# Full attention's scores copied negated out of their PSUM ring together with the maximum, with score products two slots ahead and entropy sums two slots behind

## The chip, the core and the metric

The kernel runs on one core of one Trainium2 chip. The time is the device time of one launch in microseconds (us), from the first to the last instruction of the program and what the runtime puts around them. Smaller is better. The core has five engines that run their own instruction queues in order and meet only at semaphores: TensorE (PE in the rows, its weight loads PEld), VectorE (DVE), ScalarE (ACT), GpSimd (POOL) and SyncE (SP, here the queue that issues the DMAs).

## The reference

Eight sequences of 512 tokens with 128 features pass through four residual blocks: causal attention with ALiBi, a gated feed-forward network, a second attention ("hybrid") and the feed-forward network again. The change lies in the second attention. It first needs, for all 16 heads, the whole softmax of 512 x 512 scores, only to rank the tokens:

```
scores = softmax(einsum('bhqd,bhkd->bhqk', q, k) * scale)
entropy   = -sum(scores * log(clip(scores, 1e-8)), axis=-1)
max_attn  = scores.max(axis=-1)
influence = scores.sum(axis=-2)
importance = -entropy.mean(1)*0.4 + max_attn.mean(1)*0.3 + influence.mean(1)*0.3
_, idx = top_k(importance, 51)
# then attention of all queries over the 51 picked tokens and 64 compressed ones
```

With s a score, M the maximum of its row and Z the sum of exp(s - M), the clipped logarithm of the softmax is max(s - M - ln Z, ln 1e-8). The kernel therefore forms, per query row, the sum of exp(s - M) times max(s, threshold), where the threshold is M + ln(1e-8 Z), and corrects it afterwards with a few small operations.

## The kernel before

The scores of one sequence are cut into **main tiles**: one tile is one head and one block of 128 queries, 128 partitions by 512 keys in float32, which is exactly one PSUM bank. A sequence has 16 x 4 = 64 main tiles, the eight sequences have 512. Everything in the kernel is placed on a time axis of **slots**, written out by hand in a table of constants (`FIRST`, `M_AT`, `A1_AT`, ...). Slot g holds main tile n = g - FIRST - M_AT, and beside it whatever pieces of the other stages are due: the main tiles of sequence b run while sequence b+1 is in its causal attention's second pass and its feed-forward network, b+2 in the causal first pass, and b-1 and b-2 in their small attention and last feed-forward network. The pattern thus repeats every 64 slots. Each engine walks the same slots in its own loop and waits at semaphores; no engine is bound to be in the same slot as another beyond what the semaphores ask.

For one main tile n the work is:

- TensorE, `full_scores` (L1263, product at L1268): a bf16 product into bank n % 3 of a ring of three banks (`RING`, `RN` = 3). It is issued `LEAD` = 1 slot early, that is in slot n - 1, as the first thing of that slot. From the fourth tile on it waits for `s_bn`, the semaphore of the entropy sums, of tile n - 3 (L1265).
- VectorE, first in slot n: the negated maximum of each row out of the bank, `nmB` (L1068, a TENSOR_REDUCE), which frees ScalarE's next step.
- ScalarE, in slot n: exp(s - M) out of the bank into one of eight SBUF buffers `E` (these lie in the tensor `setup`, by which the rows name them), with the sum Z as accumulator output (L827); then ln(1e-8 Z) (L830).
- GpSimd: the threshold, lnZ - nmB (L695).
- VectorE, at the end of slot n + 1, behind everything else of that slot: `entropy` (L974, operation at L978), a SCALAR_TENSOR_TENSOR that reads the scores out of the bank a second time and E from SBUF, with the sum as accumulator output. It releases the bank.
- After each fourth tile VectorE inverts Z (L1086), and one slot later TensorE adds E times 1/Z to the influence sums of the sequence (`influence`, L1271, L1276).

The other stages use banks 3, 4, 5 and 7, taken in turns that a table fixes. VectorE's parts in them are the maxima of the causal first pass (L933 to L940) and of the small attention (L946), divisions (L956, L958), residuals and layer statistics; ScalarE's are the exponentials (L813, L909), copies out of PSUM (L742) and the SiLU with its table loads (L800, L801); GpSimd's are the normalisations (L667) and the splitting of numbers into bf16 parts (L673, L678, L683, L687), all on SBUF data.

## Time and profile before

| | |
|---|---|
| median of 3 runs | 1926.42 us (1925.96 to 1930.85) |
| profiled execution, its own time | 1930.84 us |
| span of the profiled execution | 1928.7 us |
| mean granted TensorE clock | 0.692 of full speed |
| busy: PE, PE weight loads | 1487.1 us (77%), 652.0 us (34%) |
| busy: VectorE, ScalarE, GpSimd | 1223.3 us (63%), 1001.2 us (52%), 389.4 us (20%) |

Busy is the time in which an engine has an instruction in work. What is left is idle time, and the profile names for it the instruction that ended the wait. No engine is near 100%, so the waits between engines matter as much as the work. Idle time counts only on the engine that sets the pace of a stretch; which one that is changes within the 64 slots, so the profile is read by stretches of one repetition. The first main tile's maximum starts at 230 us and the last at 1779 us; before and behind lie the first sequence's earlier stages and the last one's final stages.

### The profile page before, as it was taken

To read this page: it belongs to the slowest core of one execution; us is meant where nothing else is said; L and a number is where in the kernel's file an instruction comes from. 1 tells how busy PE (TensorE), PEld (TensorE's weight loads), DVE (VectorE), ACT (ScalarE), POOL (GpSimd) and SP (SyncE) were. 2 spreads that over 40 slices of the span, in tenths; PEclk is the share of its full clock that TensorE was granted. 3 is DMA by queue.
4 is the path that set the end of the run, shared out by engine and by line. 5 is a ranking of instruction groups with operands and counts; after the bars stand their busy time and mean duration, and the time that the engine had idled before them with its cause. 6 is when DMAs were issued, how large, how long until landed. Compare 5 with 4: busy or idle time off the path is not lost.

```text
span 1928.7 us, 25028 instructions
## 1 busy us (share of the span) xinstructions
PE 1487.1 (77%) x7949; PEld 652.0 (34%) x7949; DVE 1223.3 (63%) x3203; ACT 1001.2 (52%) x2478; POOL 389.4 (20%) x900
## 2 busy tenths in 40 slices
PE   1786797888788788788788878878878878678645
PEld 1333432343334333344234333334334322321312
DVE  1503556877787477856787478857786577787211
ACT  1051376457556555656556655565654657546122
POOL 3102301330133012310233023301221012110100
PEclk9566577659666777677766876677766867665555
DMA  2110210122012110122012111211011002200100
GB/s 59 31 47 11 57 34 17 42 50 41 6 50 52 23 23 14 45 46 45 14 39 52 28 19 36 53 26 33 14 34 36 12 14 45 27 13 12 17 8 5
DMA packets 65619, 59.17 MB, mean 31 GB/s; under 512 B 11936, under 2 KB 63184, under 8 KB 65488
## 3 DMA queue, kind: packets, MB, share of 16 engines
q1 hardware_dynamic: 65488, 57.58, 14.2%
q8 instruction: 63, 1.03, 0.2%
q14 instruction: 68, 0.56, 0.1%
HBM read 39.10 MB, written 18.27 MB: 30 GB/s over the span
## 4 chain that ended last, share of the span: by engine, by line
PE 50%; DVE 22%; ACT 15%; issue 7%; POOL 3%; DMA 2%; SPq 0%; ACTq 0%; POOLq 0%; DVEq 0%
PE bank L1276 8%; PE bank L1316 7%; DVE junk L978 5%; ACT setup L827 4%; PE bank L1268 4%; PE bank L1244 3%; PE bank L1221 3%; PE bank L1299 3%; DVE nm L946 3%; ACT pT L813 2%; DVE nmB L1068 2%; DVE nm L933 2%; PE bank L1259 2%; PE bank L1251 2%; PE bank L1200 2%
## 5 line engine op out<-in xcount | busy, mean ns | idle before, releaser
L827 ACT ACTIVATE setup<-bank,nmB 128x512 f32<-128x512 f32 x512 | 350.4, 684 | 340.7 <-DVE nmB L1068 339.5
L978 DVE SCALAR_TENSOR_TENSOR junk<-bank,thr,setup 128x512 f32<-128x512 f32 x512 | 379.2, 741 | 96.5 <-POOL thr L695 92.6
L1068 DVE TENSOR_REDUCE nmB<-bank 128x1 f32<-128x512 f32 x512 | 351.1, 686 | 111.5 <-PE bank L1268 111.3
L1268 PE MATMUL bank<-k_stacks,q_stacks 48*128 48x512 bf16 x512 | 254.5, 499 | 151.8 <-DVE junk L978 150.1
L695 POOL TENSOR_TENSOR thr<-lnZ,nmB 128x1 f32<-128x1 f32 x512 | 96.7, 190 | 1223.5 <-ACT lnZ L830 1223.2
L813 ACT ACTIVATE pT<-bank 128x512 f32<-128x512 f32 x320 | 174.3, 590 | 133.5 <-PE bank L1229 132.1
L1276 PE MATMUL bank<-setup,rz 128*1 128x512 f32 x1024 | 203.0, 879 | 0.0
L1268 PEld LDWEIGHTS bank<-k_stacks,q_stacks 48*128 48x128 bf16 x512 | 49.9, 98 | 384.2 <-DVE junk L978 285.3
L1221 PE MATMUL bank<-q_stacks,k_stacks 55*128 55x384 bf16 (+3 forms) x512 | 138.9, 346 | 36.6 <-ACT pT L813 30.7
L933 DVE TENSOR_REDUCE nm<-bank 128x4 f32<-128x512 f32 x128 | 86.5, 687 | 65.8 <-PE bank L1196 65.8
L909 ACT ACTIVATE p<-bank 115x512 f32<-115x512 f32 x128 | 75.1, 587 | 81.9 <-PE bank L1435 81.8
L1435 PE MATMUL bank<-s_stacks,kcst 51*115 51x512 bf16 x128 | 76.0, 594 | 51.0 <-DVE o L958 28.4
L830 ACT ACTIVATE lnZ<-Z 128x1 f32<-128x1 f32 x512 | 103.9, 203 | 16.1
L1200 PE MATMUL bank<-k_stacks,q_stacks 52*128 52x384 bf16 (+2 forms) x384 | 96.0, 364 | 12.9 <-DVE nm L933 9.6
L1244 PE MATMUL bank<-pT,vA 128*9 128x512 f32 (+3 forms) x1024 | 104.9, 511 | 0.2 <-ACT pT L813 0.2
L1316 PE MATMUL bank<-xnT,wuT 128*128 128x512 f32 x96 | 83.0, 961 | 25.8 <-DVE gated L972 23.8
L827 ACT ACTIVATION_READ_ACCUMULATOR setup<-bank,nmB 128x1 f32 x512 | 101.8, 199 | 0.0
L667 POOL TENSOR_SCALAR xn<-x,mv,rstd 128x128 f32<-128x128 f32 x128 | 100.1, 794 | 3.3
L1229 PE MATMUL bank<-maskr,maskw 64*128 64x128 bf16 (+1 forms) x640 | 91.4, 227 | 0.0
L1192 PE MATMUL bank<-k_stacks,q_stacks 52*128 52x128 bf16 x512 | 68.4, 275 | 29.3 <-DMA k_stacks<-part_dram 17.3
L956 DVE RECIPROCAL rzo<-bank 128x16 f32<-128x16 f32 x64 | 15.7, 245 | 113.0 <-PE bank L1251 113.0
L946 DVE TENSOR_REDUCE nm<-bank 128x4 f32<-128x460 f32 x128 | 74.9, 629 | 16.2 <-PE bank L1310 15.8
(195 smaller groups left out, 2327.9 us busy)
## 6 DMA issues: line engine op xcount, KB each, us to landing
part_dram<-part SPq DMA_DIRECT2D x16, 768.0 KB, 3.2
q_stacks<-part_dram SPq DMA_DIRECT2D x192, 64.0 KB
k_stacks<-part_dram SPq DMA_DIRECT2D x192, 64.0 KB
s_stacks<-part_dram SPq DMA_DIRECT2D x48, 128.0 KB
x<-in_L_attn_a_x_dram SPq DMA_DIRECT2D x8, 256.0 KB, 7.2
x_dram<-x SPq DMA_DIRECT2D x8, 256.0 KB, 2.2
x<-x_dram SPq DMA_DIRECT2D x8, 256.0 KB, 2.9
out_dram<-x SPq DMA_DIRECT2D x8, 256.0 KB, 2.2
```

The lines of the kernel that those rows point to most:

```text
L813: act.activation(pT[:, js[0]:js[0] + len(js), c * T:c * T + WIDTH[c]], bank[3 + u % 2][:, :].rearrange("p (j q) -> p j q", j=len(js)), ACT ...
L827: act.activation(E[:, n % NE, :], RING[n % RN][:, :], ACT.Exp, bias=nmB[mb % 2][:, h, t:t + 1], accum_out=Z[mb % 2][:, h, t:t + 1]).then_i ...
L933: last = dve.tensor_reduce(nm[0][:, :, h], bank[k][:, :].rearrange("p (t k) -> p t k", t=NT), AX_X, ALU.max, negate=True)
L946: dve.tensor_reduce(nm[1][:, :, h], bank[k][:, 0:NT * NK].rearrange("p (t k) -> p t k", t=NT), AX_X, ALU.max, negate=True).then_inc(s_free ...
L978: dve.scalar_tensor_tensor(out=junk[:, :], in0=RING[n % RN][:, :], scalar=thr[mb % 2][:, h, t:t + 1], in1=E[:, n % NE, :], op0=ALU.max, op ...
L1068: dve.tensor_reduce(nmB[mb % 2][:, h, t:t + 1], RING[n % RN][:, :], AX_X, ALU.max, negate=True).then_inc(s_bm, 1)
L1200: last = pe.matmul(bank[k][:, at:at + t * P], qst[0][0:A_SC, h, t * P:(t + 1) * P], kst[0][0:A_SC, h, 0:t * P], start=True, stop=True)
L1221: pe.matmul(bank[k][:, first:first + w], kst[0][0:A_MX, h, j * P:(j + 1) * P], qst[0][0:A_MX, h, j * P:T], start=not squares, stop=True, s ...
L1244: last = pe.matmul(bank[5][QROWS * j:QROWS * j + HD + 1, k * P:T], vA[:, k, HPQ * g + j, :], pT[:, j, c * T + at:c * T + at + T - k * P], ...
L1268: pe.matmul(RING[n % RN][:, :], qst[1][0:B_SC, h, t * P:(t + 1) * P], kst[1][0:B_SC, h, :], start=True, stop=True).then_inc(s_bs, 1)
L1276: last = pe.matmul(INFL[QROWS * t:QROWS * t + 1, :], rz[mb % 2][:, h, t:t + 1], E[:, (NT * h + t) % NE, :], start=(h == 0), stop=(h == H - 1))
L1316: pe.matmul(bank[7][:, :], w, xnT[u][:, :], start=True, stop=True).then_inc(s_full[7], 1)
```

## The change

Five things are changed.

1. VectorE's first operation of a main tile becomes one TENSOR_SCALAR that reads the bank, writes the scores times -1 to one of four SBUF buffers `negs`, and leaves the minimum of them (the negated maximum, as before) as accumulator output in `nmB`. From the fifth tile on it also waits for the exponentials of tile n - 4, which read the same buffer.
2. ScalarE's exponentials and VectorE's entropy operation read `negs` from SBUF instead of the bank: the first with scale -1, the second with the minimum against a negated threshold. Signs follow in GpSimd's threshold and in two small operations for each sequence.
3. TensorE's product for tile n waits for the copy of tile n - 3, not for its entropy sum.
4. `LEAD` goes from 1 to 2: the products are issued two slots ahead.
5. The entropy operation moves from one slot behind its tile to two (`STT_LAG` = 2).

```diff
+        NS = 4
+        negs = [sb(f"negs{i}", [P, T]) for i in range(NS)]
...
-        LEAD = 1
+        LEAD = 2
+        STT_LAG = 2
...
-                        pool.tensor_tensor(thr[mb % 2][:, h, t:t + 1], lnZ[mb % 2][:, h, t:t + 1],
-                                           nmB[mb % 2][:, h, t:t + 1], ALU.subtract).then_inc(s_bt, 1)
+
+                        pool.tensor_tensor(thr[mb % 2][:, h, t:t + 1], nmB[mb % 2][:, h, t:t + 1],
+                                           lnZ[mb % 2][:, h, t:t + 1], ALU.subtract).then_inc(s_bt, 1)
...
-                        act.activation(E[:, n % NE, :], RING[n % RN][:, :], ACT.Exp, bias=nmB[mb % 2][:, h, t:t + 1],
+                        act.activation(E[:, n % NE, :], negs[n % NS][:, :], ACT.Exp, scale=-1.0,
+                                       bias=nmB[mb % 2][:, h, t:t + 1],
                                        accum_out=Z[mb % 2][:, h, t:t + 1]).then_inc(s_be, 1)
...
-                    dve.scalar_tensor_tensor(out=junk[:, :], in0=RING[n % RN][:, :], scalar=thr[mb % 2][:, h, t:t + 1],
-                                             in1=E[:, n % NE, :], op0=ALU.max, op1=ALU.mult,
+                    dve.scalar_tensor_tensor(out=junk[:, :], in0=negs[n % NS][:, :], scalar=thr[mb % 2][:, h, t:t + 1],
+                                             in1=E[:, n % NE, :], op0=ALU.min, op1=ALU.mult,
...
-                        dve.tensor_reduce(nmB[mb % 2][:, h, t:t + 1], RING[n % RN][:, :], AX_X, ALU.max, negate=True
-                                          ).then_inc(s_bm, 1)
+                        if n >= NS:
+                            dve.wait_ge(s_be, n - NS + 1)
+
+                        dve.tensor_scalar(negs[n % NS][:, :], RING[n % RN][:, :], -1.0, None, ALU.mult, ALU.min,
+                                          accum_out=nmB[mb % 2][:, h, t:t + 1]).then_inc(s_bm, 1)
...
-                    if before:
-                        entropy(*before)
+                    lagging = main_tile(g - STT_LAG)
+                    if lagging:
+                        entropy(*lagging)
...
                     if n >= RN:
-                        pe.wait_ge(s_bn, n - RN + 1)
+                        pe.wait_ge(s_bm, n - RN + 1)
```

VectorE's queue in the first main tiles of the first sequence (bank0 to bank2 are the ring, negs0 to negs3 the new buffers, Z0 and rz0 the sums and their inverses). Before:

```order
171 L978 SCALAR_TENSOR_TENSOR junk,acc0<-bank2,thr0,setup 128x512
172 L1068 TENSOR_REDUCE nmB0<-bank1 128x1
173 L1086 RECIPROCAL rz0<-Z0 128x4
174 L978 SCALAR_TENSOR_TENSOR junk,acc0<-bank0,thr0,setup 128x512
175 L1068 TENSOR_REDUCE nmB0<-bank2 128x1
176 L978 SCALAR_TENSOR_TENSOR junk,acc0<-bank1,thr0,setup 128x512
```

The same place in the changed kernel:

```order
170 L983 SCALAR_TENSOR_TENSOR junk,acc0<-negs1,thr0,setup 128x512
171 L1076 TENSOR_SCALAR negs0,nmB0<-bank1 128x512
172 L1094 RECIPROCAL rz0<-Z0 128x4
173 L983 SCALAR_TENSOR_TENSOR junk,acc0<-negs2,thr0,setup 128x512
174 L1076 TENSOR_SCALAR negs1,nmB0<-bank2 128x512
175 L983 SCALAR_TENSOR_TENSOR junk,acc0<-negs3,thr0,setup 128x512
```

Behind the inversion, tile 4 has just been read (bank1, negs0). Before, the entropy operation that follows takes tile 3, the one directly ahead; now it takes tile 2 (negs2).

TensorE's queue in the second pass of the causal attention (L1221, then L1230, are its score products, L1276, then L1285, the influence, L1244, then L1253, the weighing). Before:

```order
380 L1276 MATMUL bank6<-setup,rz0 1x512 x4
381 L1221 MATMUL bank3<-q_stacks,k_stacks 128x256 x2
382 L1229 MATMUL bank3<-maskr,maskw 128x2x64 x2
383 L1221 MATMUL bank4<-q_stacks,k_stacks 128x256 x2
384 L1229 MATMUL bank4<-maskr,maskw 128x2x64 x2
385 L1244 MATMUL bank5<-pT,vA 9x384 x4
386 L1244 MATMUL bank5<-pT,vA 9x128 x4
387 L1268 MATMUL bank0<-k_stacks,q_stacks 128x512
```

The same place in the changed kernel:

```order
380 L1277 MATMUL bank0<-k_stacks,q_stacks 128x512
381 L1285 MATMUL bank6<-setup,rz0 1x512 x4
382 L1230 MATMUL bank3<-q_stacks,k_stacks 128x256 x2
383 L1238 MATMUL bank3<-maskr,maskw 128x2x64 x2
384 L1230 MATMUL bank4<-q_stacks,k_stacks 128x256 x2
385 L1238 MATMUL bank4<-maskr,maskw 128x2x64 x2
386 L1253 MATMUL bank5<-pT,vA 9x384 x4
387 L1253 MATMUL bank5<-pT,vA 9x128 x4
388 L1277 MATMUL bank1<-k_stacks,q_stacks 128x512
```

The product into bank0 now stands ahead of a whole slot of other work that it stood behind.

## Rows read from the trace of the kernel before

**Rows 1.** The page's part 5, whole run: VectorE's two operations of a main tile and the product.

```profile
L978 DVE SCALAR_TENSOR_TENSOR junk<-bank,thr,setup 128x512 f32<-128x512 f32 x512 | 379.2, 741 | 96.5 <-POOL thr L695 92.6
L1068 DVE TENSOR_REDUCE nmB<-bank 128x1 f32<-128x512 f32 x512 | 351.1, 686 | 111.5 <-PE bank L1268 111.3
L1268 PE MATMUL bank<-k_stacks,q_stacks 48*128 48x512 bf16 x512 | 254.5, 499 | 151.8 <-DVE junk L978 150.1
```

**Rows 2.** Three stretches: busy us (count) of PE, PEld, DVE, ACT, POOL; PEclk, DMA.

```profile
1022.00:1110.00 88.00, 73.19 (x464) 35.82 (x463) 50.44 (x145) 54.87 (x134) 16.13 (x37) 0.77 0.22 44
1110.00:1154.00 44.00, 33.62 (x186) 14.56 (x186) 34.06 (x84) 25.61 (x63) 9.26 (x23) 0.75 0.12 21
1154.00:1234.00 80.00, 66.46 (x346) 27.15 (x346) 67.84 (x171) 44.14 (x114) 22.39 (x48) 0.67 0.13 30
```

**Rows 3.** The first two of these stretches for L1068 alone.

```profile
1022.00:1110.00 88.00, 16.50 (x24) 0.77 0.22 44
1110.00:1154.00 44.00, 10.98 (x16) 0.75 0.12 21
```

**Rows 4.** Waits of TensorE and VectorE from 1022 to 1110 us: total, times, longest.

```profile
PE bank L1268 <- DVE junk L978: 6.6, 3, 3.7
...
DVE nmB L1068 <- PE bank L1268: 12.8, 11, 2.5
DVE rz L1086 <- ACT setup L827: 6.1, 2, 4.6
DVE junk L978 <- POOL thr L695: 5.4, 7, 1.4
```

**Rows 5.** The same waits from 1110 to 1154 us.

```profile
PE bank L1268 <- DVE junk L978: 4.9, 4, 2.2
...
DVE junk L978 <- POOL thr L695: 3.5, 6, 1.3
...
DVE nmB L1068 <- PE bank L1268: 1.2, 1, 1.2
```

**Rows 6.** The same waits from 1154 to 1234 us.

```profile
PE bank L1268 <- DVE junk L978: 6.3, 7, 2.2
...
DVE nm L933 <- PE bank L1196: 5.9, 7, 1.9
DVE junk L978 <- POOL thr L695: 2.1, 2, 1.9
...
DVE nmB L1068 <- PE bank L1268: 1.5, 1, 1.5
```

**Rows 7.** Timeline of VectorE, two places: start us, us, then the instruction.

```profile
903.25 0.69 DVE L1068 TENSOR_REDUCE nmB<-bank 128x1 f32<-128x512 f32 x1
903.85 1.17 DVE L946 TENSOR_REDUCE nm<-bank 128x4 f32<-128x460 f32 x2
...
432.06 0.75 DVE L1011 TENSOR_SCALAR_CACHE_REDUCE hits<-bank,imp 128x512 f32<-128x512 f32 x1 [1.28 <-PE bank L1413]
...
432.75 0.35 DVE L1018 SCALAR_TENSOR_TENSOR hits<-bank,imp,tri 128x128 f32<-128x128 f32 x1
```

**Rows 8.** Groups by form: VectorE on two SBUF inputs, ScalarE from PSUM and from SBUF.

```profile
L1044 DVE SCALAR_TENSOR_TENSOR nrm<-nroot,nquot 128x128 f32<-128x128 f32 x8 | 2.3, 292 | 0.3
L742 ACT ACTIVATE xnT<-bank 128x512 f32<-128x512 f32 x32 | 18.9, 589 | 119.7 <-PE bank L1172 119.7
L768 ACT ACTIVATE part<-qf 128x512 bf16<-128x512 f32 x32 | 20.2, 630 | 1.0
```

**Rows 9.** L1141 alone (ns min/median/max), then the timeline around its run at 1025 us.

```profile
L1141 DVE TENSOR_TENSOR kw<-ktok,wt x8: 1224/1706/2076, 234.0 to 1637.9; 128x1024 f32<-128x1024 f32 x8
...
1024.94 1.14 POOL L687 TENSOR_TENSOR s_stacks<-s_stacks 16x512 bf16<-16x512 f32 x1
...
1025.15 2.08 DVE L1141 TENSOR_TENSOR kw<-ktok,wt 128x1024 f32<-128x1024 f32 x1
...
1026.05 2.19 POOL L673 TENSOR_TENSOR rest<-qf,part 128x512 f32<-128x512 f32 x1
```

More of the change, by code:

```diff
@@ L256, in hybrid_block @@
         s_bs = sem("full_scores")
-        s_bm = sem("full_maxima")
+        s_bm = sem("full_scores_copied_with_maxima")
         s_be = sem("full_exponentials")
@@ L987, in own_importance @@
                     dve.wait_ge(s_imp, 4 * b + 1)
-                    dve.scalar_tensor_tensor(out=t2[:, :, :], in0=t1[:, :, :], scalar=LOG_CLIP, in1=thr[s][:, :, :],
+                    dve.scalar_tensor_tensor(out=t2[:, :, :], in0=t1[:, :, :], scalar=-LOG_CLIP, in1=thr[s][:, :, :],
                                              op0=ALU.add, op1=ALU.subtract).then_inc(s_imp, 1)
                     dve.wait_ge(s_imp, 4 * b + 2)
-                    dve.scalar_tensor_tensor(out=t3[:, :, :], in0=t2[:, :, :], scalar=0.4 / 0.3, in1=rz[s][:, :, :],
+                    dve.scalar_tensor_tensor(out=t3[:, :, :], in0=t2[:, :, :], scalar=-0.4 / 0.3, in1=rz[s][:, :, :],
                                              op0=ALU.mult, op1=ALU.add).then_inc(s_imp, 1)
```

## The prediction, made before the result was known

> **What bounds the kernel now.** I read the busy shares first, then the groups of instructions, then the waits, and last the waits stretch by stretch. Of 1928.7 us TensorE is busy 1487 and VectorE 1223, so neither is full. The groups show the change's place: the product L1268 waits 150.1 us in all for the entropy operation L978, the maxima L1068 wait 111.3 us for the product, and L978 waits 92.6 us for GpSimd's threshold [rows 1]. That is a ring of three banks held too long: a bank comes free only when the entropy operation, one slot later and last in its slot, has read it. VectorE waits for TensorE and TensorE for VectorE by turns.
>
> These waits don't add up to a gain, since a wait removed on one engine only helps where the other has room. So I cut one repetition of 64 main tiles, from 1022 to 1234 us, into three stretches [rows 2], with 24, 16 and (the rest of 64) 24 main tiles [rows 3]. In the first, 88 us, TensorE is busy 73.2 and VectorE 50.4: TensorE sets the pace. In the second, 44 us, they are even (33.6 and 34.1). In the third, 80 us, VectorE has 67.8 and TensorE 66.5: both are near their limit.
>
> **The change, part by part.**
>
> *The copy with the maximum.* The trace has this form of operation elsewhere: L1011, from PSUM, 128x512, with accumulator output, 0.75 us against 0.69 for L1068. What counts in a full queue is the time from start to start: L1068 at 903.25 lets the next start at 903.85, 0.60 later; L1011 at 432.06 lets L1018 start at 432.75, 0.69 later [rows 7]. So it costs 0.08 us more per tile (bounds: nothing, if a constant in place of a column scalar shortens it, and 0.15, the difference of the durations with the accumulator's readout of 0.08 put behind). For 64 tiles 5 us of VectorE per repetition.
>
> *The entropy operation out of SBUF.* It was 741 ns from PSUM and SBUF with an accumulator output [rows 1]. Two float32 inputs in SBUF with an accumulator is a form the trace does not hold. The nearest are L1044 and L1141, both inputs in SBUF, no accumulator: 292 ns at 128 columns [rows 8] and 1224 ns at 1024 when undisturbed [rows 9], that is 1.04 ns per column. L978 has the same slope's worth, 0.53 of its 0.74 us. I take the duration as unchanged. The upper bound is a second pass for each column, 512 x 1.04 = 0.53 us more; the lower is 0.05 less.
>
> The row for two SBUF inputs runs at full rate, but without an accumulator. The Trainium skill, "Vector Engine (DVE) Microarchitecture Reference", section "Points that are easy to get wrong", says that a scalar-tensor-tensor operation with two non-bf16 SBUF sources has half the throughput, because both read ports are taken and none is left for the accumulator. L1044 contradicts it as far as it goes; by the page the sum would be rival D's.
>
> *VectorE against GpSimd.* This is the hidden price. L1141, two SBUF inputs, takes 1224 ns at best and 2076 at worst. In the run at 1025.15 us, GpSimd's L687 had begun at 1024.94 and ended at 1026.08; L1141 ended at 1027.23, 1.15 us after that, so it did nothing until then. GpSimd's L673, started at 1026.05, took 2.19 us and ended about 1.0 us after L1141 [rows 9]: the two exclude each other. L978 had one input in PSUM and was spared; now 512 instances can meet it. GpSimd's work beside the thresholds is 47.8 us less 64 x 0.19 of a repetition of 212 [rows 2], some 17% of the time, in pieces of about 1 us. An entropy operation meets one with that chance and waits half a piece: 0.08 us per tile on average, as an estimate. The upper bound is that VectorE stands still for all of it. In the first stretch VectorE has 37 us idle and it is hidden; in the other two it is 40 x 0.08 = 3.2 us, at most 31.6 less 40 x 0.19 = 24 us.
>
> *ScalarE* reads its exponentials from SBUF: 630 ns against 589 for a plain copy of 128x512 [rows 8], so 0.04 us more per tile, 2.6 us per repetition. ScalarE is busy 124.6 of 212 us [rows 2] and waits longest for VectorE's maxima, so I cost it at nothing; were it at its limit, 2.6 us. GpSimd's swapped subtraction and the signs cost nothing.
>
> *The bank's release and LEAD 2.* TensorE's product for tile n now needs the copy of tile n - 3, and is issued in slot n - 2, whose predecessor's copy stands first in VectorE's slot. TensorE may thus be nearly a slot further ahead, and VectorE finds its scores ready. No DMA and no other queue moves. The new waits: the copy of n waits for the exponentials of n - 4, three slots old, behind which VectorE's whole queue would stand; I expect none. The influence product stays where it was, one slot behind the inversion L1086, but its earlier guard (the entropy sum of a later tile) is gone, so it can now be the one to wait.
>
> *Entropy two slots behind.* It lets ScalarE and GpSimd be a slot late. Of the 92.6 us of waits for thresholds I expect nearly all to go. What is late next is L1086, every fourth slot, which still needs the exponentials of the tile directly ahead.
>
> **The sum, per repetition.**
> First stretch: TensorE sets the pace and waits 6.6 us for L978 [rows 4]. VectorE's own waits there, 12.8 and 5.4, lie in its slack. Gain 6.6.
> Second: VectorE loses waits of 3.5 us for thresholds and 1.2 for the product, TensorE one of 4.9 [rows 5]. VectorE gains 16 x (0.08 + 0.08) = 2.6 of work. By VectorE 2.1, by TensorE 4.9; both must get it, so 2.1.
> Third: VectorE loses waits of 2.1 and 1.5 us [rows 6] and gets 24 x 0.16 = 3.8. TensorE's 6.3 don't help, as it is then late at banks 3 and 4 as it is now (VectorE's L933 waits 5.9 for it, and it for VectorE). Gain 0.
> Together 8.7 us of 212. The eight sequences' main tiles make eight such repetitions; the last, without a causal part or a first feed-forward network beside it, is bound by VectorE throughout, and I count it as zero. 7 x 8.7 = 61 us. 1930.8 - 61 = 1870 for the profiled execution; the median of the runs shown lies 4.4 us below it, so the forecast is **1865 us**.
>
> **Rivals.**
> B, *the wait moves.* TensorE, freed of L978, waits at the influence for L1086, which waits for ScalarE: 6.1 us of such waits stand in the first stretch already, 4.6 in one piece [rows 4]. For it: that piece is not touched by the change. Against: it is one or two places of 24 slots. If it takes the first stretch's 6.6 us, 2.1 x 7 = 15 remain: 1911 us.
> C, *the exclusion costs more than average.* GpSimd's normalisations come four in a row, and a blocked VectorE delays what GpSimd is waiting for in turn. From 12 us per repetition in the last two stretches (8.7 + 3.2), half of the bound of 24, the gain is gone; at two thirds, 16 us, it is 4 us slower per repetition, 28 in all: 1954 us. For it: the second and third stretch have 31.6 of GpSimd's 47.8 us. Against: VectorE's two-input operation fills only a quarter of its time.
> D, *the entropy operation runs at half rate.* 0.53 us more for each tile. First stretch: 24 x 0.69 = 17 us fit in VectorE's 37 idle, gain 6.6 stays. Second: 16 x 0.69 - 4.7 = 6.3 slower. Third: 24 x 0.69 - 3.6 = 13.0 slower. (6.3 + 13.0 - 6.6) x 7 = 89 slower: 2015 us. For it: the form is not in the trace. Against: full rate without accumulator [rows 8], and full rate with one when one input is in PSUM [rows 1].
> E, *more is won.* All TensorE waits for L978 go and nothing follows: 150 us by rows 1 is the ceiling; two thirds of it, 100 us, would give 1826 us.
>
> **How the numbers follow.** Forecast 0.57, B 0.15, C 0.09, D 0.12, E 0.07. Within 0.3% (about 6 us, below which a measurement of this kernel can't tell a change) is "same". Faster: 0.57 + 0.07 + 0.10 of B = 0.74. Same: 0.03 of B and 0.02 of C = 0.05. Slower: D, 0.07 of C and 0.02 of B = 0.21. The forecast's own range is 1835 to 1895: gains per repetition from 4 to 13 us. The range for 8 in 10 leaves out D, part of E and the worst of C: 1818 to 1965.
>
> **What would show it.** Right: the copy near 0.75 us, the entropy operation at a minimum near 0.74 with a tail up to 1.8; waits of TensorE at the product nearly gone (150 to under 30), thresholds from 92.6 to under 20; GpSimd's long operations with a tail of 0.7 us; one repetition about 203 us. B shows as waits of the influence product for L1086's successor, C as a mean of the entropy operation above 0.9 us, D as its minimum near 1.27. The prediction is wrong if TensorE's product waits stay above 60 us, or if the repetition does not shorten although they go.

## The result, and the profile after

| | |
|---|---|
| changed kernel, median of 20 runs | 1917.99 us (1906.89 to 1935.33) |
| kernel before, median of 20 runs beside them | 1932.99 us (1924.04 to 1942.35) |
| ratio of the times, 95% interval | 0.9933 (0.991 to 0.9956) |
| profiled execution: its time, span, granted clock | 1913.95 us, 1911.8 us, 0.695 |

The change makes the kernel 0.67% faster, some 13 us, where 61 were forecast. The sign is right and the time lies in the range for 8 in 10 (1818 to 1965 us), but outside the forecast's own (1835 to 1895), and four fifths of the forecast gain are missing. Executions of one kernel differ, and the quicker ones show a higher granted clock: the changed kernel took 1935.33 us at 0.681 and 1906.89 at 0.698, some 1.7 us for each 0.001.

The page's part 1 and, from part 5, the groups of a main tile. The columns are those of [rows 1]; L983, L1076 and L1277 are the successors of L978, L1068 and L1268.

```profile
PE 1455.9 (76%) x7949; PEld 644.3 (34%) x7949; DVE 1235.0 (65%) x3715; ACT 1014.4 (53%) x2478; POOL 470.9 (25%) x900
...
L831 ACT ACTIVATE setup<-negs,nmB 128x512 f32<-128x512 f32 x512 | 367.5, 718 | 323.9 <-DVE negs L1076 322.9
L699 POOL TENSOR_TENSOR thr<-nmB,lnZ 128x1 f32<-128x1 f32 x512 | 147.5, 290 | 1124.2 <-ACT lnZ L835 1123.8
L983 DVE SCALAR_TENSOR_TENSOR junk<-negs,thr,setup 128x512 f32<-128x512 f32 x512 | 399.0, 779 | 26.6 <-POOL thr L699 26.1
L1076 DVE TENSOR_SCALAR_CACHE_REDUCE negs<-bank 128x512 f32<-128x512 f32 x512 | 350.2, 684 | 37.5 <-PE bank L1277 37.2
L1277 PE MATMUL bank<-k_stacks,q_stacks 48*128 48x512 bf16 x512 | 249.4, 494 | 30.3 <-DVE negs L1076 30.2
...
L670 POOL TENSOR_SCALAR xn<-x,mv,rstd 128x128 f32<-128x128 f32 x128 | 121.5, 961 | 3.3
```

The waits that the change aimed at went as forecast: TensorE's at the product from 150.1 to 30.2 us, the maxima's from 111.3 to 37.2, the thresholds' from 92.6 to 26.1. (The product's weight loads, which can wait while TensorE still multiplies, waited 285.3 us for the bank before and wait 110.9 now.) The copy takes 684 ns, no more than the plain maximum's 686 [rows 1]. The surprise stands in the rows of an engine that the change hardly touches: GpSimd is busy 470.9 us instead of 389.4. Its thresholds went from a mean of 190 ns to 290, its normalisations from 794 to 961.

Where the waits went, from the list of waits over the whole run (total, times, longest):

```profile
DVE rz L1094 <- ACT setup L831: 145.4, 60, 6.2
...
PE bank L1181 <- POOL xn L670: 68.8, 22, 15.3
...
PE bank L1319 <- DVE nm L951: 31.9, 36, 3.1
```

The inversion L1094 waits 145.4 us (its predecessor L1086 42.1), TensorE waits 68.8 us for the normalisations (38.7 before) and 31.9 for the small attention's maxima (15.3 before).

The smallest, middle and largest duration in ns, from the views of three single lines:

```profile
L983 DVE SCALAR_TENSOR_TENSOR junk<-negs,thr,setup x512: 709/742/2893, 237.5 to 1765.3; 128x512 f32<-128x512 f32 x171
L699 POOL TENSOR_TENSOR thr<-nmB,lnZ x512: 179/191/906, 237.2 to 1763.9; 128x1 f32<-128x1 f32 x171
L670 POOL TENSOR_SCALAR xn<-x,mv,rstd x128: 789/802/1838, 27.1 to 1883.3; 128x128 f32<-128x128 f32 x128
```

The medians are those of before. Only the tails are new, and so the means: GpSimd gained 81.5 us of busy time, the entropy operation 512 x 38 ns, some 20 us.

How the two engines meet, at 1013 us (timeline: start us, us, then the instruction):

```profile
1012.87 2.15 DVE L1149 TENSOR_TENSOR kw<-ktok,wt 128x1024 f32<-128x1024 f32 x1
...
1013.84 2.18 POOL L676 TENSOR_TENSOR rest<-qf,part 128x512 f32<-128x512 f32 x1
...
1014.94 2.89 DVE L983 SCALAR_TENSOR_TENSOR junk<-negs,thr,setup 128x512 f32<-128x512 f32 x1
...
1015.99 0.18 POOL L699 TENSOR_TENSOR thr<-nmB,lnZ 128x1 f32<-128x1 f32 x1
...
1016.13 1.14 POOL L676 TENSOR_TENSOR rest<-qf,part 128x512 f32<-128x512 f32 x1
```

The same GpSimd instruction takes 1.14 us alone and 2.18 behind L1149, which held it up until 1015.02. The entropy operation, started at 1014.94, then waited through three GpSimd instructions, until 1017.27, and lost 2.15 us. That direction, VectorE behind GpSimd, was in the forecast. It is the rarer one: 28 of the 512 entropy operations took over 10% more than their median, against 130 of the 512 thresholds and 51 of the 128 normalisations (none, 3 and 1 before). The other one, at 1121 us:

```profile
1121.20 0.74 DVE L983 SCALAR_TENSOR_TENSOR junk<-negs,thr,setup 128x512 f32<-128x512 f32 x1
...
1121.35 0.64 POOL L699 TENSOR_TENSOR thr<-nmB,lnZ 128x1 f32<-128x1 f32 x1 [4.07 <-ACT lnZ L835]
...
1123.36 3.75 POOL L670 TENSOR_SCALAR xn<-x,mv,rstd 128x128 f32<-128x128 f32 x4
...
1127.25 1.08 PE L1181 MATMUL bank<-identf,xn 128*128 128x128 f32 x4 [2.44 <-POOL xn L670]
1127.37 0.75 DVE L983 SCALAR_TENSOR_TENSOR junk<-negs,thr,setup 128x512 f32<-128x512 f32 x1 [1.09 <-POOL thr L699]
```

The entropy operation was first and takes its 0.74 us; the threshold, a single column, waits inside its own instruction until that ends. Then four normalisations, with two more entropy operations beside them, take 3.75 us (four times the undisturbed 0.79 are 3.2), TensorE waits 2.44 us for them, and the next threshold, queued behind them, keeps VectorE 1.09 us. VectorE's own row shows no loss; it comes back as a wait.

The Trainium skill, "SBUF — State Buffer", section "Who interferes with whom", calls the port pair that VectorE and GpSimd share an exclusive lock. These two timelines agree with it (2.15 us lost in one instruction, 0.45 in the other).

One repetition by the three stretches of [rows 2], cut at the same tiles (0, 24, 40, 64 of the fifth sequence), columns as there:

```profile
1007.30:1095.90 88.60, 73.99 (x468) 36.38 (x460) 52.66 (x171) 55.89 (x135) 19.97 (x38) 0.77 0.22 44
1095.90:1144.00 48.10, 38.06 (x193) 15.43 (x191) 34.57 (x103) 26.53 (x65) 11.89 (x24) 0.65 0.09 19
1144.00:1219.20 75.20, 58.99 (x343) 25.35 (x341) 67.35 (x196) 43.31 (x112) 26.58 (x46) 0.70 0.15 32
```

The first stretch, in which 6.6 of the gain's 8.7 us were to come, is not shorter, the second is 4 us longer at a lower granted clock (0.65 against 0.75), the third, for which nothing was forecast, is about 4 us shorter. Together 211.9 us: in this execution this repetition did not shorten at all. Taken as a mean over the third to fifth sequence, to which the lengths below refer too, the three stretches had 88.3, 44.6 and 78.7 us before, and 88.7, 48.0 and 75.0 after. Of the 17 us by which the profiled execution is shorter, 15 lie in the first two repetitions and ahead of them.

### The profile page after: what moved, and what is told of

Read it like the earlier page. It is cut to its first block, busy times and chain, and to the rows that moved or that the text cites. A ratio compares the mean times of both kernels' runs of the same rounds, so it can differ in the third digit from the quotient of the medians.

```text
span 1911.8 us, 26048 instructions
## 1 busy us (share of the span) xinstructions
PE 1455.9 (76%) x7949; PEld 644.3 (34%) x7949; DVE 1235.0 (65%) x3715; ACT 1014.4 (53%) x2478; POOL 470.9 (25%) x900
## 4 chain that ended last, share of the span: by engine, by line
PE 41%; DVE 24%; ACT 15%; issue 9%; POOL 7%; DMA 2%; SPq 0%; ACTq 0%; DVEq 0%; POOLq 0%
PE bank L1325 8%; PE bank L1285 6%; DVE junk L983 5%; ACT setup L831 5%; POOL xn L670 4%; PE bank L1253 3%; DVE negs L1076 3%; PE bank L1308 3%; PE bank L1230 3%; ACT pT L817 2%; PE bank L1277 2%; DVE nm L951 2%; DVE nm L938 2%; DVE nml L944 2%; PE bank L1444 2%
## 5 line engine op out<-in xcount | busy, mean ns | idle before, releaser
L831 ACT ACTIVATE setup<-negs,nmB 128x512 f32<-128x512 f32 x512 | 367.5, 718 | 323.9 <-DVE negs L1076 322.9
L699 POOL TENSOR_TENSOR thr<-nmB,lnZ 128x1 f32<-128x1 f32 x512 | 147.5, 290 | 1124.2 <-ACT lnZ L835 1123.8
L983 DVE SCALAR_TENSOR_TENSOR junk<-negs,thr,setup 128x512 f32<-128x512 f32 x512 | 399.0, 779 | 26.6 <-POOL thr L699 26.1
L1076 DVE TENSOR_SCALAR_CACHE_REDUCE negs<-bank 128x512 f32<-128x512 f32 x512 | 350.2, 684 | 37.5 <-PE bank L1277 37.2
L1277 PE MATMUL bank<-k_stacks,q_stacks 48*128 48x512 bf16 x512 | 249.4, 494 | 30.3 <-DVE negs L1076 30.2
L1285 PE MATMUL bank<-setup,rz 128*1 128x512 f32 x1024 | 201.7, 873 | 1.9 <-DVE rz L1094 1.9
L1230 PE MATMUL bank<-q_stacks,k_stacks 55*128 55x384 bf16 (+3 forms) x512 | 133.5, 334 | 41.5 <-ACT pT L817 35.0
L1277 PEld LDWEIGHTS bank<-k_stacks,q_stacks 48*128 48x128 bf16 x512 | 50.3, 101 | 241.9 <-issue 129.6
L670 POOL TENSOR_SCALAR xn<-x,mv,rstd 128x128 f32<-128x128 f32 x128 | 121.5, 961 | 3.3
L1094 DVE RECIPROCAL rz<-Z 128x4 f32<-128x4 f32 x128 | 22.1, 173 | 145.4 <-ACT setup L831 145.4
L1253 PE MATMUL bank<-pT,vA 128*9 128x512 f32 (+3 forms) x1024 | 104.0, 507 | 0.2 <-ACT pT L817 0.2
L977 DVE TENSOR_TENSOR gated<-bank,gated 128x512 f32<-128x512 f32 x48 | 33.0, 687 | 102.7 <-ACT gated L804 66.8
L831 ACT ACTIVATION_READ_ACCUMULATOR setup<-negs,nmB 128x1 f32 x512 | 97.6, 191 | 0.0
L746 ACT ACTIVATE xnT<-bank 128x512 f32<-128x512 f32 x32 | 19.0, 593 | 141.5 <-PE bank L1181 141.4
```

Source lines behind the costliest of these rows:

```text
L670: last = pool.tensor_scalar(xn[:, t, :], xs[u][:, t, :], mv[u][:, t, 0:1], rstd[u][:, t:t + 1], ALU.subtract, ALU.mult)
L699: pool.tensor_tensor(thr[mb % 2][:, h, t:t + 1], nmB[mb % 2][:, h, t:t + 1], lnZ[mb % 2][:, h, t:t + 1], ALU.subtract).then_inc(s_bt, 1)
L831: act.activation(E[:, n % NE, :], negs[n % NS][:, :], ACT.Exp, scale=-1.0, bias=nmB[mb % 2][:, h, t:t + 1], accum_out=Z[mb % 2][:, h, t:t ...
L983: dve.scalar_tensor_tensor(out=junk[:, :], in0=negs[n % NS][:, :], scalar=thr[mb % 2][:, h, t:t + 1], in1=E[:, n % NE, :], op0=ALU.min, op ...
L1076: dve.tensor_scalar(negs[n % NS][:, :], RING[n % RN][:, :], -1.0, None, ALU.mult, ALU.min, accum_out=nmB[mb % 2][:, h, t:t + 1]).then_inc( ...
L1230: pe.matmul(bank[k][:, first:first + w], kst[0][0:A_MX, h, j * P:(j + 1) * P], qst[0][0:A_MX, h, j * P:T], start=not squares, stop=True, s ...
```

## The experiments

All times below are ratios to the kernel before, run beside each, with the 95% interval. To compare two experiments I subtract ratios and take 1933 us as the whole. Three theories were open. X: the copy puts a second SBUF input on VectorE, and the exclusion with GpSimd eats the gain. Y: the waits only moved, to the inversion. Z: the engines' own work (VectorE's, TensorE's, ScalarE's) sets the time, and waits were never worth much. In the expectations T2 is, by and large, X, T1 is Y and T3 is Z for VectorE; each text spells out what they mean for its kernel.

Where two kernels also differ in their mean granted clock, a part of the difference in time can be the clock's, and no run here shows why the clock differs.

### Parts of the change alone

The first kernel has the products one slot ahead, the second the entropy sums one slot behind, the third both, so that the copy with its early release stands alone.

```
-        LEAD = 2
+        LEAD = 1          # first and third kernel
-        STT_LAG = 2
+        STT_LAG = 1       # second and third kernel
```

> The changed kernel with LEAD back at 1, entropy sums still two slots behind. Theory T1 (the removed waits only moved, mostly to the inversion L1094, so that no single early start is worth much): VectorE's waits for the product go from 37 us back to about 100, the inversion's waits shrink by as much, time within 4 us of the changed kernel, ratio to before 0.992 to 0.996. Theory T2 (the gain of 15 us comes from the products standing ahead, the rest is eaten by VectorE and GpSimd excluding each other): the gain goes, ratio 0.998 to 1.004.

Measured: 0.9913 (0.9879 to 0.9947), with 183.4 us of waits of the copies for their products and 68.6 at the inversion. T2 of this text falls.

> The changed kernel with STT_LAG back at 1, products still two slots ahead. T1: waits for thresholds go from 26 us back to about 90, and the waits at the inversion fall from 145 to about 60, since both wait for the same exponentials of the tile directly ahead; time within 4 us of the changed kernel (ratio 0.992 to 0.996). T2: the lag is worth something of its own, since the exclusion makes thresholds late: 10 to 20 us slower than the changed kernel, ratio 0.999 to 1.004.

Measured: 0.9969 (0.9943 to 0.9994), between the two ranges, with 162.1 us of waits for thresholds and 55.4 at the inversion.

> The copy and the early release of the bank alone: LEAD 1 and STT_LAG 1. T1: part of the product's waits (150 us before) still go, to about 60, threshold waits at about 90, time 3 to 8 us under before (ratio 0.996 to 0.999). T2: the exclusion costs more than the early release gives; slower than before by 5 to 15 us, ratio 1.003 to 1.008.

Measured: 0.9924 (0.9885 to 0.9962), better than either range. The first and the third lie as low as the full change's 0.9933; the second's interval overlaps with it. So the copy with its early release is the whole gain, and neither lead nor lag adds to it that these runs could tell (no kernel was run with the copy but with the old, late release, so that the two are not told apart). In the third kernel TensorE waits only 4.5 us for the copy: its 150.1 us went by the release alone. What lead and lag remove are waits of VectorE, which in the third kernel waits 114.7 us for products, 97.0 for thresholds and 39.0 at the inversion. In the full change they are 37.2, 26.1 and 145.4: 148 us went and 106 came back at the inversion. Whether the 148 us cost nothing or only moved (Y), these kernels can't tell. Two rows of the third kernel's page:

```profile
L983 DVE SCALAR_TENSOR_TENSOR junk<-negs,thr,setup 128x512 f32<-128x512 f32 x512 | 409.8, 800 | 101.1 <-POOL thr L699 97.0
...
L1277 PE MATMUL bank<-k_stacks,q_stacks 48*128 48x512 bf16 x512 | 240.9, 482 | 4.6 <-DVE negs L1076 4.5
```

### One SBUF input in the entropy operation

The entropy operation loses its scores and keeps length, threshold, order, waits and accumulator, so that only the second SBUF input goes.

```
-  dve.scalar_tensor_tensor(out=junk, in0=negs[n % NS], scalar=thr, in1=E[n % NE], op0=ALU.min, op1=ALU.mult, accum_out=acc)
+  dve.tensor_scalar(junk, E[n % NE], thr, None, ALU.min, ALU.add, accum_out=acc)
```

> The changed kernel with the entropy operation replaced by a one-input form of the same width (min of E with the threshold, summed; the scores are left out of it, so the picked tokens and the output differ), with the same waits. It takes VectorE's second SBUF input away and with it the exclusion against GpSimd. GpSimd's busy time should fall from 471 to about 390 us, its normalisation from 0.96 to 0.79 us, the waits of TensorE for it from 69 to about 40. T2 (the exclusion ate the gain): 25 to 45 us faster than the changed kernel, ratio to before 0.970 to 0.980. T1 (the removed waits moved, TensorE and its clock set the repetition): within 6 us of it, 0.990 to 0.996.

Measured: 0.9705 (0.9681 to 0.9729), median 1879.64 us. Its page, part 1 and the rows that answer:

```profile
PE 1451.2 (77%) x7949; PEld 638.2 (34%) x7949; DVE 1212.9 (65%) x3715; ACT 1014.4 (54%) x2478; POOL 389.6 (21%) x900
...
L983 DVE TENSOR_SCALAR_CACHE_REDUCE junk<-setup,thr 128x512 f32<-128x512 f32 x512 | 376.0, 734 | 19.4 <-POOL thr L699 18.6
...
L699 POOL TENSOR_TENSOR thr<-nmB,lnZ 128x1 f32<-128x1 f32 x512 | 97.0, 190 | 1173.3 <-ACT lnZ L835 1173.1
...
L670 POOL TENSOR_SCALAR xn<-x,mv,rstd 128x128 f32<-128x128 f32 x128 | 100.2, 795 | 3.3
```

GpSimd is back at 389.6 us, its two rows are those of before, and the operation's median is 736 ns against 742, so its work is worth at most 512 x 6 ns = 3 us. The kernel is 0.0228 or 44 us (about 6 us either way) faster than with two inputs. That is theory X's. The inversion still waits 140.9 us, so Y has nothing to do with these 44 us. A part of them came with a higher clock, 0.696 in the mean against 0.690: the executions at 0.695 alone took 1881 to 1884 us against 1913.95 with two inputs, so that 30 to 33 us remain at an equal clock.

The same edit on the copy alone, lead and lag 1:

> One SBUF input in the entropy operation (the scores left out of it, output differs) with LEAD 1 and STT_LAG 1. It separates the two halves of the change without the exclusion. If LEAD and the lag are worth what the prediction gave them once nothing collides: 20 to 40 us slower than the run with one SBUF input alone, ratio to before 0.980 to 0.992. If the copy's early release is all, as it was with the exclusion (0.9924 without both): within 8 us of it, 0.968 to 0.975.

Measured: 0.9651 (0.9605 to 0.9698), 0.0273 or 53 us (about 12 either way) below its partner with two inputs, and better than either range. Here too the clock was higher (0.707 in the mean against 0.694): at 0.704 to 0.707 the two take 1870.90 and 1872.49 us against 1900.96 and 1900.15, 28 to 30 us. Without the exclusion the early release is thus worth 57 to 67 us, what came with the clock included. Where it is lost shows in the stretches, here of the one-input kernel at full lead and lag:

```profile
985.20:1070.70 85.50, 73.76 (x470) 34.57 (x463) 50.10 (x173) 56.07 (x135) 17.21 (x38) 0.78 0.21 45
1070.70:1114.80 44.10, 33.99 (x190) 14.80 (x191) 33.85 (x103) 26.30 (x65) 9.46 (x24) 0.72 0.08 21
1114.80:1189.10 74.30, 58.89 (x339) 24.75 (x341) 66.93 (x194) 43.23 (x111) 21.12 (x46) 0.68 0.11 33
```

Mean lengths over three sequences of the profiled executions, which lie only 28 to 32 us apart, are 84.2, 43.2 and 74.7 us (83.9, 42.0 and 76.6 with the copy alone). Against two inputs the first stretch loses 4.5 and 4.0 us, the second 4.8 and 1.3, the third nothing (0.3 and -0.3). Of the second's 4.8, TensorE's busy time has 4 (38.06 against 33.99) at a granted clock of 0.65 against 0.72, so that this part need not be the exclusion's own.

### The inversion

Its wait for the exponentials of the tile directly ahead is moved one slot later, with the influence product behind it.

```
-        INFL_LAG = 5
+        INFL_LAG = 6
-                    before = main_tile(g - 1)      # the inversion
+                    before = main_tile(g - 2)
```

> The changed kernel with the inversion of the four sums, and the influence product behind it, one slot later (INFL_LAG 6). T1: the wait of 145 us at the inversion falls under 30 and most of it is real: 15 to 35 us faster than the changed kernel, ratio to before 0.975 to 0.985. T2: the wait only moves on (to the entropy sums' thresholds and the banks of the other stages); within 4 us of the changed kernel, ratio 0.991 to 0.996.

Measured: 0.9889 (0.9848 to 0.993), between the two ranges and overlapping with the change's interval. The inversion's waits fell from 145.4 to 27.4 us, and the time by 0.0044 or 9 us (about 9 either way). But the edit does more than remove a wait. ScalarE's copy of a sequence's influence sums (L899) stayed in its slot, while the last influence product moved one slot later, so that ScalarE now waits for it in each of the eight sequences. The changed kernel, then this one:

```profile
ACT infl L899 <- PE bank L1285: 4.0, 1, 4.0
```

```profile
ACT infl L899 <- PE bank L1285: 52.4, 8, 7.9
```

The 9 us are what is left of both, and not the price of the inversion's waits. No kernel was run with that copy moved along.

> LEAD 1, entropy sums two slots behind, inversion and influence product one slot later. By the runs so far the early product is worth nothing (0.9913 without it, 0.9933 with it) and the later inversion perhaps 0.4%. If the two are independent: ratio to before 0.985 to 0.990, the best so far. If both only move the same wait: 0.990 to 0.993.

Measured: 0.9995 (0.9967 to 1.0022), outside both ranges and slower than either edit alone (by 0.0082 than with lead 1). The copies wait 196.4 us for products, but so they do, 183.4, with lead 1 alone. New against lead 1 is ScalarE's wait for the influence product, 49.5 us instead of 3.7; but it is as long in the kernel before this one, which was not slower. It stays open.

> One SBUF input (output differs) with the inversion and the influence product one slot later. If the 141 us of VectorE's waits at the inversion hold the first stretch, which the prediction had 6.6 us shorter: repetition down from about 202 to 195 us, ratio to before 0.950 to 0.962. If those waits lie in slack: 0.966 to 0.974.

Measured: 0.9804 (0.9752 to 0.9856), outside both ranges and slower than the one-input kernel by 0.0099 (about 0.0057 either way). The inversion's waits fell from 140.9 to 25.5 us, and ScalarE's for the influence product rose from 4.0 to 52.7. So moving the inversion in this way gives nothing that could be relied on, and costs something in two of three kernels. For theory Y that leaves two things: it is no account of the 44 us, and whether the inversion's waits are why lead and lag give nothing is not shown, since each of these edits put a new wait on ScalarE.

### Less work on one engine

A quarter of the entropy operation's columns (128 of 512):

> The changed kernel with the entropy operation on 128 of 512 columns (three quarters of the entropy sum left out). VectorE has 0.40 us less to do in each of 512 tiles, 205 us in all. T1 with TensorE as the bound: at most 25 us faster than the changed kernel, ratio to before 0.980 to 0.993. T3 (VectorE sets the pace of half of each repetition, as the prediction had it for the third stretch): 60 to 100 us faster, ratio 0.945 to 0.965.

Measured: 0.9514 (0.9485 to 0.9544), 81 us faster than the change, with VectorE busy 1038.3 us instead of 1235.0. GpSimd is nearly free of the exclusion too (397.4 us), which by the one-input kernel is 44 of the 81. The other 37 are what some 175 us less work on VectorE gives, a fifth of it; the mean clock was also higher, 0.706 against 0.690, and no run separates the two. That is theory Z's part, and a small one.

A quarter of the influence product's columns:

> The changed kernel with the influence products on 128 of 512 columns (three quarters of the influence sum left out). TensorE has about 0.6 us less for each of 512 tiles at the present clock, some 150 us of its busy time of 1456. T1 with TensorE as the bound: 70 to 130 us faster than the changed kernel, ratio to before 0.93 to 0.96. T3: under 40 us faster, since VectorE then holds the second and third stretch, ratio 0.97 to 0.99.

Measured: 0.9816 (0.9785 to 0.9847), 0.0117 or 23 us faster. The stretch from 600 to 1400 us, of this kernel and then of the changed one, columns as in [rows 2]:

```profile
600.00:1400.00 800.00, 657.53 (x3843) 323.41 (x3842) 581.59 (x1773) 482.83 (x1181) 212.73 (x413) 0.65 0.16 35
```

```profile
600.00:1400.00 800.00, 649.03 (x3791) 293.39 (x3790) 578.39 (x1742) 475.21 (x1163) 214.77 (x407) 0.72 0.17 34
```

The influence product was busy 68.2 us instead of 201.7, and TensorE as a whole no less than with it, since the granted clock stood at 0.65 instead of 0.72 (0.626 against 0.695 over the whole run); its score product took 533 ns instead of 494. So of 133.5 us of work taken off one product, TensorE's busy time shows nothing and the kernel's time 23 us.

### Work off GpSimd

The layer normalisations, which GpSimd did as (x - mean) x rstd, go to ScalarE. GpSimd keeps two operations of four columns each for the bias.

```
-  pool.tensor_scalar(xn[:, t, :], xs[u][:, t, :], mv[u][:, t, 0:1], rstd[u][:, t:t + 1], ALU.subtract, ALU.mult)
+  pool.tensor_tensor(nb[u], negm[u], rstd[u], ALU.mult)
+  act.activation(xn[:, t, :], xs[u][:, t, :], ACT.Identity, bias=nb[u][:, t:t + 1], scale=rstd[u][:, t:t + 1])
```

On the changed kernel:

> The changed kernel with the four normalising operations of each layer norm moved from GpSimd to ScalarE (scale 1/std, bias -mean/std; one slot after GpSimd's statistics), all else as it is. GpSimd loses 121 us of work that reads SBUF. T2 (VectorE and GpSimd excluding each other cost 44 us, as the run with one SBUF input had it): about half of that comes back, 15 to 35 us faster than the changed kernel, ratio to before 0.974 to 0.986. If instead the exclusion at the thresholds is what costs, under 6 us, 0.990 to 0.996. ScalarE gets some 40 us of work, which it has room for; if not, slower.

Measured: 0.986 (0.9813 to 0.9907). On the kernel before, as a control:

> The kernel before with the same move, as the control: it has no operation of two SBUF inputs on the main tiles, so nothing to win from less exclusion. T2: within 8 us of before, ratio 0.996 to 1.004. If the gain of the move came from a shorter way through the layer norm instead, it would show here as well: 0.98 to 0.99.

Measured: 0.9982 (0.9946 to 1.0018). The move is worth 0.7% (14 us, about 10 either way) on the changed kernel, and nothing that can be told on the one before: that is what X asks for, though the two gains differ by no more than their errors. The kernel with the copy alone, further below, makes the difference clear: there the move gives 0.0129 or 25 us (about 12 either way). So where the entropy operation excludes GpSimd it matters that GpSimd has less to do in SBUF; the move recovers a third of the 44 us here, and half of the 53 there.

The thresholds instead, written by ScalarE behind its logarithm, alone and with the normalisations:

```
-  pool.tensor_tensor(thr, nmB, lnZ, ALU.subtract)
+  act.activation(thr, lnZ, ACT.Identity, bias=nmB, scale=-1.0)
```

> The changed kernel with the thresholds computed on ScalarE behind the logarithm (0.2 us more for each tile there) and no longer on GpSimd. GpSimd loses 147 us of small operations, half of them spent blocked. If the exclusion at the thresholds is what costs (they go from 190 to 290 ns): 15 to 30 us faster than the changed kernel, ratio to before 0.977 to 0.986. If GpSimd's long operations are: within 6 us, or slower by ScalarE's 100 us of added work in its full stretch, 0.990 to 1.000.

Measured: 1.004 (1.0005 to 1.0074), slower than either range.

> Both moves together: GpSimd keeps only the splitting into bf16 parts and the statistics. T2: near the 0.9705 of the run with one SBUF input, 0.965 to 0.980, and the best version that computes everything. If ScalarE's added 140 us weigh: 0.985 to 1.000.

Measured: 0.9958 (0.9926 to 0.9991). Both are slower than without the edit, by 0.0107 and 0.0098: it puts 150.8 us (512 x 294 ns) into ScalarE's queue between one tile's exponentials and the next. What the exclusion costs through the thresholds alone can't be read from it.

### Complete kernels that use this

The normalisations on ScalarE with the later inversion, and with the copy alone (lead and lag 1):

> The whole computation, normalisation on ScalarE (0.986 alone), inversion one slot later (0.989 alone). If independent: 0.978 to 0.984, the best complete version. If both act on the same wait: 0.984 to 0.989.

Measured: 0.9852 (0.9808 to 0.9895), no better than without the inversion's edit. ScalarE's new wait for the influence product is here too, 52.3 us.

> The whole computation, normalisation on ScalarE, LEAD 1 and STT_LAG 1. By the copy alone (0.9924) and the move (0.7% on the changed kernel): 0.983 to 0.990; if the move needs the products two slots ahead to pay: 0.990 to 0.997.

Measured: 0.9795 (0.9749 to 0.9841), median 1899.74 us. It computes all that the reference asks and has the lowest ratio of such kernels, 2.05% below the kernel before and 0.0138 below the change (about 0.005 either way), though its interval overlaps with those of 0.9852 and 0.986. It lies below both ranges of the expectation: the move gives 0.0129 here against 0.0073 on the full change, with errors that overlap. Its threshold, from its page:

```profile
L698 POOL TENSOR_TENSOR thr<-nmB,lnZ 128x1 f32<-128x1 f32 x512 | 128.8, 252 | 1195.5 <-ACT lnZ L844 1195.0
```

At a mean of 252 ns against 190 undisturbed, the exclusion is still there.

## Why the prediction was right or wrong

**Right: the mechanism of the early release.** 150 to 30.2 us at the product ("under 30" was asked), 92.6 to 26.1 at the thresholds ("under 20"): both nearly as forecast. The release by the copy took the first away (4.5 us with the copy alone), lead and lag those of VectorE for products and thresholds, which were not what paid, as the kernels without them show.

**By its own sign, wrong.** The prediction called itself wrong "if the repetition does not shorten although they go". The product's waits went, and in the profiled execution the repetitions of the third to fifth sequence take 211.6 to 211.9 us against 211.6 before.

**Right: full rate from two SBUF inputs.** Minimum 709 and median 742 ns, against 741 from PSUM [rows 1] and 1270 by rival D, which falls. The Trainium skill, "Vector Engine (DVE) Microarchitecture Reference", section "Points that are easy to get wrong", has half the throughput for this form; the measurement decides against it.

**Wrong on the safe side: the copy.** 0.08 us per tile was added. It was none: 684 ns, and the next instruction starts 0.61 us after the copy's start (L1076 at 880.97, L961 at 881.58), as behind the plain maximum [rows 7], with the accumulator's readout beside it:

```profile
880.97 0.69 DVE L1076 TENSOR_SCALAR_CACHE_REDUCE negs<-bank 128x512 f32<-128x512 f32 x1
881.58 0.08 DVE L1076 DVE_READ_ACCUMULATOR negs<-bank 128x1 f32 x1
881.58 0.25 DVE L961 RECIPROCAL rzo<-bank 128x16 f32<-128x16 f32 x1
```

**The step that failed: "VectorE against GpSimd".** The prediction called it the hidden price and then sized it as "0.08 us per tile on average", VectorE's wait alone, "hidden" in the first stretch for VectorE's 37 us of idle time, 3.2 us per repetition in the other two, so 22 us in all. Three things were wrong with that. VectorE's average itself was too high: 38 ns, 20 us in the whole run. The exclusion works both ways, and the far larger part fell on GpSimd, 81.5 us. And "hidden" was asked of the wrong engine: the idle time of VectorE does not cover a late normalisation, for which TensorE now waits 68.8 us instead of 38.7, nor what hangs on a late threshold. So the loss came in the first stretch, 4.0 to 4.5 us of 6.6 forecast as gain, and not in the third. In the whole kernel it is 44 us (full change) or 53 (copy alone), not 22; at an equal clock some 30, still more than 22.

**The other term mis-sized: the gain itself.** By the prediction's own terms the sum without the exclusion is 8.7 + 3.2 = 11.9 us per repetition or 83 in all; measured without it, 57 and 67. Some 16 to 26 us of the waits that were counted as gain were thus not on the path, or came back elsewhere. In the first stretch, where 6.6 us should go, the one-input kernels gained 4.1 and 4.4; most likely the pace passes to ScalarE and the inversion there, but the runs only show that waits appear at both. The second gave 1.4 and 2.6 (forecast 2.1, without the exclusion 3.4), and the third, for which nothing was forecast, 4.0 and 2.1, through which waits no run shows.

**The rivals.** Of B, the move of the wait is there and larger than thought, 42.1 to 145.4 us, at the inversion itself and not where B put it, at the influence product (1.9 us); its price stays open, since the kernels with the later inversion bring a wait of their own. C had the right cause, but its place, the last two stretches, and its sign were wrong: 44 to 53 us are 6 to 8 per repetition, where C asked for 12 to 16, and as VectorE standing still; by its own sign, a mean above 0.9 us, it falls (0.779). E is far off. So the likeliest had the release right, which pays some 60 us where the exclusion is gone. That 57 to 67 us is also the forecast's number is luck: without the exclusion the forecast's own sum is 83.

**What stays open.** The steady repetition has 211.6 us (to 211.9) before and after, with lag 1, and with lead 1 and the later inversion, in the profiled executions, at different waits; the granted clock's rows differ by stretch (0.75 to 0.65 in the second) in a way that gives back what is won, but no run shows why. Open too are why the later inversion costs 0.0082 and 0.0099 in two kernels and nothing in two others, with the same new wait of ScalarE in all four; what the inversion's waits are worth; whether the part of the 44 to 53 us above 30 is the exclusion's or the clock's; and how they divide between thresholds and normalisations.

## What to carry to other kernels

Before PSUM data is copied to SBUF so that a two-input VectorE operation no longer holds its bank, look at what GpSimd does beside it, and cost the exclusion on both engines: first who waits for GpSimd, then who waits for VectorE. Keep one of the inputs in PSUM or move GpSimd's SBUF work to ScalarE, if that has room. And try an early release alone before adding leads and lags, since a large sum of waits that goes away proves no gain: here most of it came back at the next wait. When one step is moved a slot later to test its wait, look for the step behind it that now waits instead.

## What the runs showed of the hardware

- A single-column GpSimd operation of 190 ns is delayed as a long one is, up to 906 ns, by a VectorE operation of 742 ns with two SBUF inputs. A VectorE operation can wait through several GpSimd instructions in a row (2893 ns in one piece).
- Neither the copy from PSUM to SBUF nor a clipped sum with one input in SBUF and its output there disturbs GpSimd: 389.6 us busy against 389.4 before.
- TENSOR_SCALAR with an accumulator, 128x512 float32 from PSUM to SBUF, takes 684 ns, as the reduction without an output does. The same form at L1011 took 0.75 [rows 7]; what makes the difference no run shows.
- ScalarE's exponentials with an accumulator take 718 ns from SBUF; from PSUM they took 684.
- Three quarters of the influence product less left TensorE's busy time where it was, with the granted clock at 0.626 instead of 0.695.
